# A decoder's cross-attention pieces beside its gated attention: the pairs of pieces moved by one

## The chip, the cores and the metric

The kernel runs on one core of one Trainium2 chip. The metric is the device time of one execution in microseconds (us), the median of the runs shown. The core's engines are TensorE (PE in the profile, PEld its weight loads), VectorE (DVE), ScalarE (ACT), GpSimd (POOL) and SyncE (SP), which issues the transfers. Each runs its own instructions in program order and meets the others at semaphores.

## The reference

A decoder of two layers on 8 sequences of 256 tokens, width 512, all float32. Each layer is attention, cross-attention to a context, and experts, each followed by a residual sum and a layer norm:

```python
x = _layernorm(x + _L0_attn_ref(x, Wq, Wk, Wv, Wg, Wc, bc))
x = _layernorm(x + _L0_xattn_ref(x, ctx_2048, ctx_2048))
x = _layernorm(x + _L0_ffn_ref(x, ...))
...
```

The change touches the first two. The first (called A here) squares the scores of 16 query heads and weights them by a gate, in blocks of 256 tokens here (one per sequence):

```python
qk = jnp.einsum("bthd,bshd->bhts", q, k) * scale
a = jnp.where(causal, qk ** 2 * jnp.exp(gate), 0.0)
y = jnp.einsum("bhts,bshd->bthd", a, v) / (jnp.sum(a, axis=-1) + 1e-06)
out = y.reshape(B, T, H * R * D) @ Wc + bc
```

The second (called C) has 16 heads of width 32, and takes the context as keys and values without a projection:

```python
scores = jnp.einsum("bhqd,bhkd->bhqk", q, kj) * SCALE
scores = jnp.where(causal, -inf, scores)
exp_c = jnp.exp(scores - scores.max(axis=-1, keepdims=True))
out = jnp.einsum("bhqk,bhkd->bhqd", exp_c / exp_c.sum(axis=-1, keepdims=True), vj)
```

## The kernel before

The program is seven stages: constants, `attention0` (A), `cross0` (C), and four more. A and C are written as generators: each engine's part of the stage yields after every tick, and `decoder` deals the ticks out by a list `order` of (stage, number of ticks). `in_order` (L159) runs that list for the banks of PSUM and for each of the five engines, so the list sets the order of work on every engine at once. No scheduler moves anything afterwards.

**A** has 32 steps n (8 pairs of heads, 4 groups of 512 tokens, in two halves) and two more that drain it. A step has 8 ticks on TensorE: three projections `project(n, m)` (L384, 12 matmuls each; ScalarE copies the high part qkH at L561, VectorE the rest qkL at L684); then two ticks of `out(n-2, ...)` (L417, 12 matmuls each, added to xN by VectorE at L653); then `attend(n-1)` (L434 to L439), in three late steps of the stage with 96 matmuls of values (L457) behind it; then `scores(n)` (L471, L473; ScalarE squares them at L597, VectorE multiplies them by the gate at L710); then `turn(n-1)` (eight transpositions at L486; ScalarE takes the high part yH at L605, VectorE the rest yL at L722). ScalarE also exponentiates the gates (L572) behind the third projection, and in every second step copies the next weights there (L575).

**C** has 8 batches j of 8 pieces i, a piece being two heads, and 16 ticks to a batch: 144 ticks in all, from -8 to 135. On an even tick 16j + 2i stand the scores of piece i, on the odd tick after it the transpositions of its exponentials. What belongs to a piece:

- `scores(j, i)`, TensorE L946: 12 matmuls into two banks. They wait until ScalarE has read the piece whose banks they take.
- VectorE L1061: four instructions that add the mask and take the maxima (each followed by a read of the accumulator).
- ScalarE L1030 and L1032: four exponentials into P, of which there is one copy (also with accumulator reads).
- `flip(j, i)`, TensorE L958: six transpositions of P, which wait for the exponentials, and for both banks 6 and 7.
- ScalarE L1040: the copy of the transposed P into PT.
- `attend(j, g)`, TensorE L929: once in two pieces, on the even ticks 4, 8, 12 and 16 of a batch ahead of the scores of that tick: 16 narrow matmuls of PT with the context. It waits for the copy (L1040) of the flip on the tick just before it. ScalarE copies the result at L1017.

Three times or less in a batch an even tick has more behind its scores: `turn` (L978, four transpositions of xN, ticks 16j - 6 and 16j + 6; ScalarE L1009, VectorE L1072) and `finish` (L968, tick 16j + 18; VectorE L1087). They too put their result into bank 6 or 7. The keys of C are split on GpSimd (L1119, L1121), and its context is loaded by SyncE.

Steps 0 to 16 of A run alone with all eight banks. From step 17 on A has banks 0 to 3, and C has 4 and 5 for scores and 6 and 7 for the rest: after every four ticks of A (behind the first out tick, and behind turn) come two of C, 66 in all. These places are called the half after out and the half after turn. What is then left of A and C follows, C alone:

```python
A, C, done = 1, 2, 0
order = [(0, 1), (A, 1 + 8 * 17)]
for n in range(17, 34):
    for ticks in (4, 4):
        beside = min(2, 66 - done)
        order += [(A, ticks), (C, beside)]
        done += beside
order += [(A, 2), (C, c0.ticks - done)]
```

Of the kernel before, what the change touches and what calls it, by code (L numbers as in the profile page):

```python
# [144 lines left out]
def whole(stage):  # L145

    def once(f):
        def pieces(e):
            f(e)
            yield  # L150
        return pieces

    def banks():
        yield

    return Stage(1, banks, *(once(f) for f in stage))


def in_order(order, pieces):  # L159
    for s, n in order:  # L160
        for _ in range(n):
            next(pieces[s])
    for s in pieces:
        assert next(s, None) is None
# [85 lines left out]
def constants(K):  # L250

    def gpsimd(e):
        step = K.steps(e, "pool_step")
        e.memset(K.onesF[:, :], 1.0)
        e.memset(K.onesel[:, :, :], 0.0)
        step(e.memset(K.idF[:, :], 0.0))
        step(e.affine_select(out=K.idF[:, :], in_=K.idF[:, :], compare_op=ALU.not_equal, fill=1.0, base=0,
                             pattern=[[-1, 128]], channel_multiplier=1))
        e.tensor_copy(K.idB[:, :], K.idF[:, :])
        for i in range(4):  # L260
            last = e.memset(K.onesel[:, i, i:i + 1], 1.0)
        last.then_inc(K.consts.sem, 1)

    nothing = lambda e: None
    return nothing, nothing, nothing, gpsimd, nothing
# [2774 lines left out]
def decoder(nc, d, out):  # L3040
    with ExitStack() as ctx:
        K = Kit(nc, ctx, d, out)
        first = whole(constants(K))
        a0 = attention0(K, 17)
        c0 = cross0(K)
        K.rooms, rooms = Rooms(), K.rooms
        rest = [whole(stage(K)) for stage in (experts0, attention1, cross1, experts1)]
        stages = [first, a0, c0, *rest]

        A, C, done = 1, 2, 0  # L3050
        order = [(0, 1), (A, 1 + 8 * 17)]
        for n in range(17, 34):
            for ticks in (4, 4):
                beside = min(2, 66 - done)
# [3 lines that stand above are left out]
        order += [(i, 1) for i in range(3, 7)]  # L3058

        block = ctx.enter_context(nc.Block())  # L3060
        in_order(order, [s.banks() for s in stages])

        @block.tensor
        def _(e):
            in_order(order, [s.engines[0](e) for s in stages])

        @block.scalar
        def _(e):
            in_order(order, [s.engines[1](e) for s in stages])

        @block.vector
        def _(e):
            in_order(order, [s.engines[2](e) for s in stages])

        @block.gpsimd
        def _(e):
            in_order(order, [s.engines[3](e) for s in stages])

        @block.sync
        def _(e):  # L3080
            in_order(order, [s.engines[4](e) for s in stages])
# [48 lines left out]
```

## Time and profile before

| | us |
|---|---|
| median of 2 runs | 2661.53 (2659.25 to 2663.8) |
| the profiled execution | 2657.87 |
| its span, first to last instruction | 2656.1 |
| TensorE busy in the span | 2206.7 (83%) |
| A alone (steps to 16) | about 25 to 430 |
| A and C together; the first transposition of exponentials starts at 470.0 | about 430 to 991 |
| C alone | about 991 to 1275 |

1.8 us of the profiled execution lie outside of its span. Times in the rows are microseconds from the start of the span. The granted clock is TensorE's, as a share of 2.4 GHz: 1.00 is that level, 0.50 is 1.2 GHz, and a value between is a mean over a stretch that had both. "Idle before" is the time for which the engine did nothing ahead of an instruction, with the instruction of another engine that ended it. Matmuls overlap: one has a duration of its own, but the next starts before it ends, so that a group's busy time is less than count times duration. A row of a stretch begins with its limits and length; then, engine by engine (PE, PEld, DVE, ACT, POOL), busy us and the count of instructions; then the granted clock, the share of the DMA engines and GB/s. For one line alone only PE and PEld stand there. A row of a timeline has the start, the us from the first start to the last end of the instructions merged in it, and the instruction.

### The profile page before, as it was taken

The page shows a single profiled execution, that of the slowest core. Times are in us where ns is not written, and L with a number is a line of the kernel's source. Part 1 is how long each engine was busy: PE and PEld are TensorE (multiplying, and loading weights), DVE is VectorE, ACT ScalarE, POOL GpSimd, SP SyncE. Part 2 cuts the span into 40 slices and gives each one's busy share as a digit, 9 for nine tenths or more (in the row PEclk, how much of TensorE's full clock was granted, in tenths as well). Part 3 has the DMA queues.
Part 4 walks back from the last instruction along what each step waited for, and adds up shares of the span by engine and source line. Part 5 has one row for each costly group of instructions (what it writes and reads, how often), then busy time and mean ns, then how long its engine had stood idle before and what let it go on. Part 6 is the DMA issues. An engine that isn't in the chain of part 4 may idle for free.

```text
span 2656.1 us, 37210 instructions
## 1 busy us (share of the span) xinstructions
PE 2206.7 (83%) x13669; PEld 1754.7 (66%) x13669; DVE 1251.9 (47%) x3209; ACT 1044.3 (39%) x2330; POOL 744.3 (28%) x668
## 2 busy tenths in 40 slices
PE   6999998877878865555789999998899978888774
PEld 6788887766767653444678888886665536666542
DVE  2644456333343343232531111333677767677655
ACT  3333233333333334333322111123466656777632
POOL 2734343223222210010024343003435432232110
PEclk9999999888888885555999999999899988999986
DMA  4211111011011000000100100001323330000001
GB/s 154 97 45 30 58 48 64 26 32 47 16 40 32 11 15 16 18 17 3 52 32 30 42 33 0 24 1 22 66 45 59 58 105 21 13 25 8 2 9 63
DMA packets 53173, 98.52 MB, mean 37 GB/s; under 512 B 6913, under 2 KB 31233, under 8 KB 50177
## 3 DMA queue, kind: packets, MB, share of 16 engines
q1 hardware_dynamic: 52992, 96.14, 12.7%
q8 instruction: 110, 1.80, 0.3%
q14 instruction: 71, 0.57, 0.1%
HBM read 75.61 MB, written 4.26 MB: 30 GB/s over the span
## 4 chain that ended last, share of the span: by engine, by line
PE 39%; issue 9%; DVE 8%; ACT 6%; POOL 2%; DMA 1%; SPq 0%; ACTq 0%; DVEq 0%; POOLq 0%
PE PS L1253 13%; PE PS L1325 3%; PE PS L1352 3%; PE PS L1736 2%; PE PS L1832 2%; PE PS L958 2%; PE PS L946 2%; DVE aM L1969 1%; PE PS L1800 1%; ACT xP L2494 1%; DVE st L191 1%; ACT cP L1032 1%; PE PS L2346 1%; PE PS L929 1%; ACT cP L1030 1%
## 5 line engine op out<-in xcount | busy, mean ns | idle before, releaser
L958 PE MATMUL PS<-idF,cP 128*128 128x128 f32 x384 | 94.3, 416 | 203.3 <-ACT cP L1032 186.9
L958 PEld LDWEIGHTS PS<-idF,cP 128*128 128x128 f32 x384 | 70.8, 215 | 219.2 <-issue 135.3
L1253 PE MATMUL PS<-WH,bXH 128*128 128x512 f32 x512 | 201.2, 393 | 5.4 <-POOL WL L1546 5.4
L1253 PE MATMUL PS<-WL,bXH 128*128 128x512 f32 x512 | 200.7, 392 | 0.0
L1253 PE MATMUL PS<-WH,bXL 128*128 128x512 f32 x512 | 200.7, 392 | 0.0
L1969 DVE TENSOR_REDUCE aM<-PS 128x4 f32<-128x1024 f32 x128 | 153.8, 1221 | 57.4 <-PE PS L1800 56.5
L1061 DVE CUSTOM_DVE_ANT_0 PS<-PS,cBAR 128x128 f32<-128x128 f32 (+1 forms) x256 | 83.7, 389 | 187.2 <-PE PS L946 187.2
L1456 DVE SCALAR_TENSOR_TENSOR s<-s,cf,PS 128x256 f32<-128x256 f32 x112 | 53.8, 481 | 249.0 <-ACT s L1371 240.0
L384 PE MATMUL PS<-aXH,QKH 128*128 128x512 f32 x384 | 162.4, 423 | 6.7 <-ACT sq L597 3.4
L684 DVE TENSOR_TENSOR qkL<-PS,qkH 128x512 fp32r<-128x512 f32 x96 | 65.8, 690 | 203.2 <-ACT qkH L561 203.2
L1371 ACT ACTIVATE s<-PS 128x256 f32<-128x256 f32 x128 | 49.0, 383 | 277.4 <-PE PS L1253 277.4
L384 PE MATMUL PS<-aXL,QKH 128*128 128x512 f32 x384 | 157.9, 411 | 0.0
L384 PE MATMUL PS<-aXH,QKL 128*128 128x512 f32 x384 | 156.9, 409 | 0.0
L653 DVE TENSOR_TENSOR xN<-PS,xN 128x512 f32<-128x512 f32 x128 | 88.3, 691 | 142.3 <-PE PS L417 139.1
L1908 ACT ACTIVATE aPT<-PS 128x1024 f32<-128x1024 f32 x128 | 128.6, 1024 | 50.7 <-PE PS L1820 49.7
L1561 POOL TENSOR_TENSOR mixed<-mixed,s 128x256 f32<-128x256 f32 x112 | 82.4, 739 | 183.3 <-DVE s L1456 183.3
L2494 ACT ACTIVATE xP<-PS,xM 128x256 f32<-128x256 f32 x256 | 118.0, 483 | 28.9 <-DVE xM L2616 28.9
L561 ACT ACTIVATE qkH<-PS 128x512 fp32r<-128x512 f32 x96 | 56.9, 598 | 173.9 <-PE PS L384 173.9
L710 DVE TENSOR_TENSOR aT<-sq,E 128x512 f32<-128x512 f32 (+1 forms) x128 | 88.6, 733 | 77.0 <-ACT sq L597 48.0
L597 ACT ACTIVATE sq<-PS 128x768 f32<-128x768 f32 x64 | 51.9, 811 | 163.8 <-PE PS L473 108.9
L417 PE MATMUL PS<-CH,yH 128*128 128x512 f32 x256 | 112.4, 439 | 3.4 <-DVE qkL L684 3.4
L1253 PEld LDWEIGHTS PS<-WH,bXH 128*128 128x128 f32 x512 | 97.0, 189 | 25.3 <-issue 5.5
(405 smaller groups left out, 6294.5 us busy)
## 6 DMA issues: line engine op xcount, KB each, us to landing
gQK<-in_Wqk SPq DMA_DIRECT2D x16, 768.0 KB, 6.3
gC<-in_Wc SPq DMA_DIRECT2D x16, 512.0 KB, 5.4
lgB<-gate_sums SPq DMA_DIRECT2D x32, 256.0 KB, 4.2
sg<-in_gu SPq DMA_DIRECT2D x8, 1024.0 KB, 5.0
aqs<-aQH SPq DMA_DIRECT2D x64, 128.0 KB, 4.3
xN<-in_xT SPq DMA_DIRECT2D x4, 1024.0 KB, 10.7
xN<-in_x SPq DMA_DIRECT2D x4, 1024.0 KB, 7.6
cst<-in_cT SPq DMA_DIRECT2D x8, 512.0 KB, 3.7
```

Of the source, the lines that this page charges most:

```text
L384: mm = e.matmul(PS[:, b, :], w[:, kc, 128 * m:128 * m + 128], x[:, kc, c:c + 512], start=kc == 0 and i == 0, stop=kc == KC - 1 and i == 2)
L417: mm = e.matmul(PS[:, b, :], y[:, h, 128 * i:128 * i + 128], w[:, h, :], start=h == 0 and k == 0, stop=h == 1 and k == 2)
L653: e.tensor_tensor(xN[:, t, :], PS[:, b, :], xN[:, t, :], ALU.add).then_inc(o_add.sem, 1)
L710: at = e.tensor_tensor(aT[:, j, c:c + w].rearrange("p (h q) -> p h q", h=2), sq[:, c:c + w].rearrange("p (h q) -> p h q", h=2), E[:, j:j + ...
L958: mm = e.transpose(PS[:, b + a, 128 * c:128 * c + 128], P[:, a, c, :], idF[:, :])
L1061: last_ = e.tensor_tensor_reduce(out=s, in0=s, in1=BAR[:, 256 - 128 * q:384], scale=1.0, scalar=3.0e38, op0=ALU.add, op1=ALU.min, accum_ou ...
L1253: mm = e.matmul(PS[:, b, :], x[:, kc, 128 * t:128 * t + 128], w[:, kc, :], start=kc == 0 and i == 0, stop=kc == KC - 1 and i == 2)
L1325: mm = e.matmul(PS[:, b + a, :], x[:, kc, 128 * t:128 * t + 128], w[:, kc, :], start=kc == 0 and i == 0, stop=kc == KC - 1 and i == 2)
L1561: e.tensor_tensor(mixed[:, t, :], mixed[:, t, :], s2[n % 2][:, 0:256], ALU.add).then_inc(t_add.sem, 1)
L1908: e.activation(PT[:, n % 8, :, :], PS[:, b:b + 2, :], ACTF.Exp, scale=0.25).then_inc(t_exp.sem, 1)
L1969: e.tensor_reduce(M[j % 2][:, :, :].rearrange("x q (h c) -> x h q c", h=2)[:, :, :, i], PS[:, b:b + 2, :].rearrange("p h (q k) -> p h q k" ...
L2494: last = e.activation(P[:, i % 2, a, q, :], PS[:, r, 256 * q:256 * q + 256], ACTF.Exp, bias=M[y][:, q, h:h + 1], scale=-1.0, accum_out=den ...
```

## The change

The list of ticks changes in two places. One tick of C (its first, -8) is placed ahead of step 17 of A, and the count of ticks placed starts at 1. So each pair of C ticks within the stage now begins with an odd tick: the transposition of piece i (with what its tick holds), then the even tick with the attend, if there is one, and the scores of piece i + 1. There are 32 pairs and one single tick instead of 33 pairs, 66 ticks as before. An even tick comes one half of a step of A earlier than before, an odd tick in the same half. No instruction is added or taken away.

```diff
-        A, C, done = 1, 2, 0
-        order = [(0, 1), (A, 1 + 8 * 17)]
+        A, C, done = 1, 2, 1
+        order = [(0, 1), (A, 1 + 8 * 17), (C, 1)]
         for n in range(17, 34):
             for ticks in (4, 4):
                 beside = min(2, 66 - done)
```

TensorE in the half after turn, before: the turn of A, the scores of a piece, its own flip, the first projection of A's next step.

```order
L486 MATMUL PS<-idF,yN 128x128 x8
L946 MATMUL PS<-cKH,cQH 128x128 x2
L946 MATMUL PS<-cKL,cQH 128x128 x2
L946 MATMUL PS<-cKH,cQL 128x128 x2
L946 MATMUL PS<-cKH,cQH 128x256 x2
L946 MATMUL PS<-cKL,cQH 128x256 x2
L946 MATMUL PS<-cKH,cQL 128x256 x2
L958 MATMUL PS<-idF,cP 128x128 x6
L384 MATMUL PS<-aXH_52,QKH 128x512
```

The same engine and place after the change.

```order
L486 MATMUL PS<-idF,yN 128x128 x8
L958 MATMUL PS<-idF,cP 128x128 x6
L929 MATMUL PS<-cPT,cV 32x256 x4
L929 MATMUL PS<-cPT,cV 32x128 x4
L946 MATMUL PS<-cKH,cQH 128x128 x2
L946 MATMUL PS<-cKL,cQH 128x128 x2
L946 MATMUL PS<-cKH,cQL 128x128 x2
L946 MATMUL PS<-cKH,cQH 128x256 x2
L946 MATMUL PS<-cKL,cQH 128x256 x2
L946 MATMUL PS<-cKH,cQL 128x256 x2
```

The flip moved ahead of the scores, and is now that of the piece before. The attend (L929), which stood in the half after out, came to the half after turn, right behind the flip whose copy it reads.

ScalarE around the same place, before: A's squares and yH, the exponentials of the piece, the copy of its flip, then A's qkH of the next step.

```order
L597 ACTIVATE sq<-PS 128x768 x2
L605 ACTIVATE yH<-PS 128x512 x2
L1030 ACTIVATE cP,cden_96<-PS,cM_94 128x128
L1032 ACTIVATE cP,cden_96<-PS,cM_94 128x256
L1030 ACTIVATE cP,cden_96<-PS,cM_94 128x128
L1032 ACTIVATE cP,cden_96<-PS,cM_94 128x256
L1040 ACTIVATE cPT<-PS 128x768
L561 ACTIVATE qkH<-PS 128x512 x3
```

ScalarE there after the change.

```order
L597 ACTIVATE sq<-PS 128x768 x2
L605 ACTIVATE yH<-PS 128x512 x2
L1040 ACTIVATE cPT<-PS 128x768
L1017 ACTIVATE cnT<-PS 128x256
L1030 ACTIVATE cP,cden_96<-PS,cM_94 128x128
L1032 ACTIVATE cP,cden_96<-PS,cM_94 128x256
L1030 ACTIVATE cP,cden_96<-PS,cM_94 128x128
L1032 ACTIVATE cP,cden_96<-PS,cM_94 128x256
L561 ACTIVATE qkH<-PS 128x512 x3
```

The copy L1040 moved ahead of the exponentials, with L1017 behind it; both stay behind A's squares and yH.

TensorE in the half after out, in a pair whose even tick has a finish, after the change: the end of A's first out tick, the flip, the scores, and the finish (L968) behind them; the next row is A's second out tick.

```order
L417 MATMUL PS<-CH,yL 128x512
L958 MATMUL PS<-idF,cP 128x128 x6
L946 MATMUL PS<-cKH,cQH 128x128 x2
L946 MATMUL PS<-cKL,cQH 128x128 x2
L946 MATMUL PS<-cKH,cQL 128x128 x2
L946 MATMUL PS<-cKH,cQH 128x256 x2
L946 MATMUL PS<-cKL,cQH 128x256 x2
L946 MATMUL PS<-cKH,cQL 128x256 x2
L968 MATMUL PS<-idF,cnT 128x128 x8
L417 MATMUL PS<-CH,yH 128x512
```

All turns and finishes of C within the stage stand in this half now, behind a flip whose banks 6 and 7 they take one of.

## Rows read from the trace of the kernel before

**Rows 1.** The page: span, busy time, TensorE and its granted clock in 40 slices.

```profile
span 2656.1 us, 37210 instructions
PE 2206.7 (83%) x13669; PEld 1754.7 (66%) x13669; DVE 1251.9 (47%) x3209; ACT 1044.3 (39%) x2330; POOL 744.3 (28%) x668
...
PE   6999998877878865555789999998899978888774
...
PEclk9999999888888885555999999999899988999986
```

**Rows 2.** Busy time by stretch: A alone, both together, C alone.

```profile
200.00:430.00 230.00, 227.69 (x1295) 197.67 (x1293) 118.17 (x230) 74.63 (x117) 97.40 (x79) 1.00 0.16 48
...
467.00:989.00 522.00, 412.90 (x2456) 346.28 (x2453) 204.20 (x560) 172.49 (x426) 127.43 (x107) 0.87 0.09 28
989.00:1260.00 271.00, 155.22 (x1000) 114.37 (x998) 80.69 (x373) 102.02 (x345) 24.73 (x24) 0.51 0.04 13
```

**Rows 3.** Waits from 467 to 989: total us, times, longest.

```profile
PE PS L958 <- ACT cP L1032: 96.1, 26, 6.2
...
PE PS L958 <- DVE coN L1087: 11.9, 3, 4.0
```

**Rows 4.** Busy time by stretch of one line alone: L384, then L417, then L958.

```profile
200.00:430.00 230.00, 86.24 (x360) 66.80 (x360) 1.00 0.16 48
467.00:989.00 522.00, 118.53 (x432) 93.55 (x432) 0.87 0.09 28
...
200.00:430.00 230.00, 59.76 (x255) 47.43 (x253) 1.00 0.16 48
467.00:989.00 522.00, 104.68 (x340) 79.14 (x341) 0.87 0.09 28
...
467.00:989.00 522.00, 41.30 (x174) 30.85 (x174) 0.87 0.09 28
```

**Rows 5.** Timeline of one half after turn: start, us, instruction.

```profile
564.72 1.04 PE L486 MATMUL PS<-idF,yN 128*128 128x128 f32 x8
...
565.69 0.33 PE L946 MATMUL PS<-cKH,cQH 32*128 32x128 f32 x2
...
566.29 1.08 ACT L605 ACTIVATE yH<-PS 128x512 fp32r<-128x512 f32 x2
566.36 0.28 PE L946 MATMUL PS<-cKH,cQL 32*128 32x256 f32 x2
...
568.63 0.29 DVE L1061 CUSTOM_DVE_ANT_0 PS<-PS,cBAR 128x128 f32<-128x128 f32 x1
...
570.60 0.48 ACT L1032 ACTIVATE cP<-PS,cM 128x256 f32<-128x256 f32 x1
...
571.31 1.48 PE L958 MATMUL PS<-idF,cP 128*128 128x128 f32 x6 [4.08 <-ACT cP L1032]
...
573.02 0.63 PE L384 MATMUL PS<-aXL,QKH 128*128 128x512 f32 x1
...
575.46 0.39 PE L384 MATMUL PS<-aXH,QKL 128*128 128x512 f32 x1
```

**Rows 6.** Timeline: the waits of two flips in the half after out.

```profile
660.23 1.51 PE L958 MATMUL PS<-idF,cP 128*128 128x128 f32 x6 [2.74 <-ACT cP L1032]
...
860.98 1.04 PE L958 MATMUL PS<-idF,cP 128*128 128x128 f32 x6 [2.74 <-ACT cP L1032]
```

**Rows 7.** C alone: the waits of the attends, and a flip, its copy and its attend.

```profile
PE PS L929 <- ACT cPT L1040: 18.1, 18, 1.0
...
1063.97 0.81 ACT L1040 ACTIVATE cPT<-PS 128x768 f32<-128x768 f32 x1 [1.75 <-PE PS L958]
1064.88 1.51 PE L929 MATMUL PS<-cPT,cV 128*32 128x256 f32 x16 [1.01 <-ACT cPT L1040]
```

**Rows 8.** Timeline of a half after out: ScalarE's last work of A, the attend.

```profile
617.85 1.48 ACT L575 ACTIVATE QKH<-gQK 128x1536 fp32r<-128x1536 f32 x1
...
619.14 0.86 PE L929 MATMUL PS<-cPT,cV 128*32 128x256 f32 x16
```

## The prediction

> **What bounds the kernel now.** The page comes first: TensorE is busy for 83% of the span, more than any other engine, but its row of slices has a dip from the eighth slice on, and the row of the granted clock has eights in the same slices, where it had nines before [rows 1]. A slice is 66 us, so that is where A and C run together. The view by stretches says it in numbers. In A alone TensorE is busy for 227.7 of 230 us at a clock of 1.00; from 467 to 989 us it is busy for 412.9 of 522 us at 0.87; in C alone for 155.2 of 271 us at 0.51 [rows 2]. In the middle stretch VectorE has 204, ScalarE 172 and GpSimd 127 us of work in 522, so none of them is full. What TensorE waits for there stands in the view of waits: the flips, L958, for ScalarE's exponentials, 96.1 us in 26 waits, and for VectorE's coN, 11.9 us in 3 [rows 3]. That is 108.0 us in 29 waits, one for each of the 174 / 6 = 29 flips of the stretch [rows 4]. Nothing else of size stands in the way.
>
> The timeline of one half shows why. The scores end at about 566.64 us. VectorE is still at A's work and starts the maxima at 568.63; the last exponential ends at 570.60 + 0.48 = 571.08; only then does the flip go, after 4.08 us of idle [rows 5]. In the half after out VectorE is free and the wait is 2.74 us [rows 6]. Every piece thus pays a trip through VectorE and ScalarE in full, though TensorE has A's work ready behind it.
>
> **What the waits cost beside themselves.** Behind such a wait matmuls of A take 0.63 us, some microseconds later 0.39 us again [rows 5]: these are the two levels of the clock, 1.2 and 2.4 GHz. I price it from busy time for each matmul. L384: 118.53 / 432 = 0.274 us in the middle stretch against 86.24 / 360 = 0.240 in A alone, times 432: 15 us. L417: 104.68 / 340 = 0.308 against 59.76 / 255 = 0.234, times 340: 25 us. The flips: 41.30 / 29 = 1.42 us each, against 1.04 for one at the full level, times 29: 11 us [rows 4, 6]. Together 51 us, or 1.8 us for each wait.
>
> **What the change removes.** The flip of piece i now stands four ticks of A behind its scores. The trip took 571.08 - 566.64 = 4.4 us with VectorE's backlog in it [rows 5]. The cover after the half after turn is three projections and an out tick: 48 matmuls at 0.23 us, 11 us. After the half after out it is an out tick, 12 x 0.234 = 2.8 us, and A's attend, scores and turn. In A alone 360 / 36 = 10 steps left (227.7 - 86.2 - 59.8) / 10 = 8.2 us each for these three and the values [rows 2, 4]; about half of it is theirs, so the cover is some 7 us. Both exceed 4.4 us, and the 7 us still do with the copy of the flip (0.81) added, which ScalarE now makes before the exponentials [rows 7]. So the 29 waits go, 108 us. At the end of the stage A's steps are short: its last two have no projections, and a flip there has only an out tick of 2.8 us as cover. I leave 2 us for this (bounds 0 and 6, two waits of 2.74 us [rows 6]).
>
> **What it adds: the attend behind its flip.** Before, the attend began its pair and found the copy of the last flip long done; it starts at 619.14 with no idle ahead of it [rows 8]. Now flip, copy and attend follow one another. C alone has this very order, and there each attend waits, 18.1 us in 18 waits, 1.0 us each, with TensorE's flips at the lower clock [rows 7]. Beside A it is worse, for all attends have come to the half after turn, where ScalarE has A's yH before the copy. Step by step from rows 5: turn ends at 564.72 + 1.04 = 565.76; a flip at the full level then ends at about 566.7 (the 1.04 of rows 6, begun while the turn drains); yH ends at 566.29 + 1.08 = 567.37; the copy takes 0.81 and the attend starts 0.10 after it (1064.88 - 1063.97 - 0.81) [rows 7]: 568.3. The wait is 1.6 us. Attends stand on every fourth tick from 4 to 56, 14 of them: 22 us. Bounds: 14 x 1.0 = 14 us, as in C alone, and 14 x 2.4 = 34 us if ScalarE is a square (0.8 us) later than in the row. Behind the waiting attend are queued the scores and then A's projections; ScalarE's exponentials and VectorE's maxima wait for these scores, but nothing needs them before the next half.
>
> **What it adds: banks 6 and 7.** The 7 turns and 3 finishes of C in the stage now stand behind a flip and 12 matmuls of scores (565.69 to 566.64, 0.95 us), and need a bank that the copy frees [rows 5]. In the half after out ScalarE is free at 617.85 + 1.48 = 619.33 at the latest, before the flip would end at about 620.0 [rows 8]. The copy ends 0.9 us after the flip (0.10 + 0.81), so against 0.95 us of scores little is left: 0.4 us each with a second hop, 4 us in 10 (bounds 0 and 10 us).
>
> **What it adds: lags in A.** ScalarE's exponentials now fall into A's first projection. With the attend from 568.3 on (0.8 us until the scores start) and 0.95 us of scores, these end at about 570.1. From the first maximum to the last exponential it took 571.08 - 568.63 = 2.45 us [rows 5], so ScalarE is free at about 572.7. The projection ends at 570.1 + 2.8 = 572.9, and qkH is not late. That is 0. But the margin is 0.2 us, and a denser TensorE leaves less slack in steps with norms and values. The other bound is VectorE's backlog in the row, 568.63 - 566.64 = 2.0 us, in each of 17 steps: 34 us. I stay near the row that I followed, and take 6 us.
>
> The transfers move by half a step with their ticks, against batches of 16 ticks; SyncE's and GpSimd's items of C come no later relative to those who need them. At nothing: GpSimd's 127 us of work in 522 leave it room [rows 2]. If a key load came late, TensorE would wait at the scores.
>
> **The clock after the change.** Waits of 2.74 us and more were followed by the lower level; whether 1.6 us are is not shown. Bounds: never, 0 us, or each as dear as now, 14 x 1.8 = 25 us. The place has only short matmuls around the wait (turn, flip, attend, scores), so I take half, 12 us. Of the 51 us, 39 come back.
>
> On the flips themselves the rows are plain: of two flips after the same wait one took 1.51 us and one 1.04 us, so transpositions do run at the upper level [rows 6]. The Trainium skill, "TensorE: Matmul & The Clock Gate", section on PE-mode transpose, speaks against a gain here: it says that the full clock does not engage for transpositions. By that rule flips would stay at 1.51 us, and the change would return 11 us less; by the rows it returns them. The trace disagrees with the page, and I go by the trace.
>
> **The sum.** 108 + 51 = 159 us are there to win. Taken back: attends 22, banks 6 and 7 4, the end of the stage 2, A's lags 6, clock 12, together 46. The gain is 113 us. C alone and all later stages keep their order and their time. Against the profiled execution: 2657.87 (span 2656.1 and 1.8 around it) - 113 = 2544.9 us. The median of the runs is 3.7 us above that execution, so 2661.53 - 113 = 2548.5, and I predict 2548 us. All terms at their good ends give 108 + 51 - 14 = 145 us, 2517; at their bad ends 159 - 34 - 10 - 6 - 34 - 25 = 50 us, 2611. All bad at once is unlikely; the likeliest case alone spans 2522 to 2590.
>
> **Rivals.** *The clock stays down.* The wait of 1.6 us stands between transpositions and narrow matmuls, and a lower level may follow each time and last twice as long as now. For it: in C alone, made of the same instructions, the clock is 0.51 throughout [rows 2]. Against it: 11 us of dense matmuls follow each time. Price: 14 x 3.6 = 50 us instead of 12: 2548 + 38 = 2586 us.
>
> *The attend hardly waits.* If ScalarE is through with yH when the flip ends, each attend waits 1.0 us as in C alone, the clock stays up, and banks and lags cost nothing: 159 - 14 - 2 = 143 us, 2518. For it: the one row of this place that I followed need not be typical. Against it: rows 5, where the copy cannot start before 567.37.
>
> *The wait only moves.* A's projections find their banks not free, since qkH and qkL come behind the exponentials in both engines' queues, and L384 or L417 wait as long as L958 did. Then only the 4 ticks' distance is spent, and the time is 2661 less some 10: 2650. For it: just four banks. Against it: 7 and 11 us of cover over a trip of 4.4.
>
> *Slower.* The same mechanism at full strength, and the attend's wait on top. Place: A's out blocks, which wait for qkL's bank. Price: all 108 + 51 us stay, plus 14 x (1.6 + 1.8) = 48 us: 2661 + 48 = 2709. It decides once the lag per half exceeds the cover of at least 7 us by more than 3.7 us, a trip of about 11 us, more than double the 4.4 of rows 5. It would need a queue that I do not see.
>
> **Chances.** The forecast 0.74, the clock staying down 0.13, the attend hardly waiting 0.08, the wait moved 0.03, slower 0.02. The range takes in the first three cases nearly whole: 2515 to 2595 us. What a measurement can tell from no change is about 2%, 53 us, so faster means below 2608: all of the first three cases, 0.95; same is the moved wait, 0.03; slower 0.02.
>
> **What would show it.** Right: in the stretch of A and C together, now about 410 us long instead of 522, waits of L958 for cP near nothing; 14 waits of L929 for cPT of about 1.6 us; a mean clock of 0.95 or more; L384 near 0.24 us of busy time for each matmul; the stretch of C alone still 271 us. The first rival shows as a clock under 0.92 with the waits gone, the second as waits of L929 near 1.0 us, the third as waits of L384 or L417 for sq, qkL or xN of over 2 us in each half. The forecast is wrong if flips still wait, if C alone grows, or if some other line waits for over 30 us in sum.

## The result, and the profile after

| | before | after |
|---|---|---|
| median of the runs | 2661.53 (2 runs) | 2530.47 (2529.7 to 2531.25) |
| ratio, 95% interval | | 0.9508 (0.9467 to 0.9549) |
| the same with more runs, on another chip | 2649.86 (7 runs) | 2530.27 (4 runs), 0.9548 (0.9534 to 0.9563) |
| span of the profiled execution | 2656.1 | 2528.0 |

The forecast was 2548 us with a range of 2515 to 2595. The gain is 131 us in the first comparison and 120 in the second: the kernel before is at 2650 to 2655 us in all later comparisons, and the changed one at 2530 in both.

The page of the changed kernel, the rows that answer to [rows 1]:

```profile
span 2528.0 us, 37196 instructions
PE 2157.2 (85%) x13655; PEld 1717.9 (68%) x13669; DVE 1247.5 (49%) x3209; ACT 1043.3 (41%) x2330; POOL 746.3 (30%) x668
...
PE   7899999999899755657899999997999877888774
...
PEclk9999999999999955559999999997999999999886
```

The eights in the clock before its four fives are gone, and TensorE's row has nines, with one eight, up to the place where C is alone. By stretch, against [rows 2]:

```profile
200.00:430.00 230.00, 227.08 (x1291) 196.84 (x1290) 118.29 (x230) 74.44 (x117) 97.91 (x78) 1.00 0.15 48
430.00:860.00 430.00, 397.14 (x2592) 335.51 (x2592) 218.62 (x586) 179.19 (x435) 142.59 (x121) 0.98 0.12 39
...
867.00:1130.00 263.00, 149.35 (x976) 110.26 (x978) 77.84 (x368) 102.01 (x345) 23.16 (x22) 0.51 0.05 14
```

A alone is the same. Where both run, TensorE is busy for 92% instead of 79% of the time, and its clock is 0.98 instead of 0.87. C alone is the same, at 0.51. The view of one line gives first and last start of its instructions, and so the ends of the stages: A's last out block, and C's last attend.

```profile
L417 PE MATMUL PS<-CH,yL x256: 388/389/398, 88.5 to 866.8; 128*128 128x512 f32 x128
...
L929 PE MATMUL PS<-cPT,cV x512: 271/421/635, 477.4 to 1130.5; 128*32 128x128 f32 x86, 128*32 128x256 f32 x85
```

Before, A's last matmul started at 991.8 and C's last attend at 1255.4. So A ends 125.0 us earlier (866.8), C alone takes 263.7 us instead of 263.6, and everything behind it takes 1397.5 instead of 1400.7 us. Of the 128.1 us between the two spans 125.0 were made where the change is. TensorE's whole work from 430 us to the end of A's last out block, before and then after:

```profile
430.00:992.20 562.20, 448.22 (x2624) 374.95 (x2624) 227.10 (x610) 186.68 (x449) 142.02 (x122) 0.88 0.10 30
```

```profile
430.00:867.20 437.20, 403.93 (x2624) 340.52 (x2624) 223.65 (x608) 184.55 (x448) 142.59 (x121) 0.98 0.12 39
```

The same 2624 matmul records take 44.3 us less of busy time, and the idle time falls from 114.0 to 33.3 us, 80.7 less: together the 125.0 us.

All waits of TensorE for another engine from 430 to 867 us, against [rows 3]:

```profile
PE PS L929 <- ACT cPT L1040: 27.6, 14, 3.4
...
PE PS L384 <- ACT sq L597: 1.4, 1, 1.4
PE PS L434 <- DVE xN L653: 1.3, 1, 1.3
PE PS L417 <- DVE qkL L684: 1.1, 1, 1.1
PE PS L486 <- DVE yN L664: 0.8, 1, 0.8
PE PS L958 <- ACT cP L1032: 0.2, 1, 0.2
```

Of 108 us of waits of the flips 0.2 are left. In their place stand 14 waits of the attends. One half after turn, against [rows 5]:

```profile
567.28 1.03 PE L486 MATMUL PS<-idF,yN 128*128 128x128 f32 x8
568.15 0.82 PE L958 MATMUL PS<-idF,cP 128*128 128x128 f32 x6
568.18 0.81 ACT L597 ACTIVATE sq<-PS 128x768 f32<-128x768 f32 x1 [1.15 <-DVE aT L710]
...
568.88 1.08 ACT L605 ACTIVATE yH<-PS 128x512 fp32r<-128x512 f32 x2
...
569.84 0.83 ACT L1040 ACTIVATE cPT<-PS 128x768 f32<-128x768 f32 x1
...
570.77 0.86 PE L929 MATMUL PS<-cPT,cV 128*32 128x256 f32 x16 [1.80 <-ACT cPT L1040]
571.55 0.33 PE L946 MATMUL PS<-cKH,cQH 32*128 32x128 f32 x2
```

The flip goes at once and is done at 568.97. ScalarE has A's square and yH ahead of the copy, which ends at 570.67, and the attend starts 0.10 us later: 1.80 us of wait. Of the 14, eleven are 1.76 to 1.94 us, two 3.43, and the last 1.01.

Busy time of one line alone by stretch, L384, L417 and L958, against [rows 4]:

```profile
430.00:860.00 430.00, 125.69 (x504) 98.81 (x504) 0.98 0.12 39
...
430.00:860.00 430.00, 88.52 (x360) 66.37 (x360) 0.98 0.12 39
...
430.00:860.00 430.00, 22.91 (x168) 19.59 (x168) 0.98 0.12 39
```

For each matmul that is 0.249 us in L384 (0.274 before, 0.240 in A alone) and 0.246 in L417 (0.308 and 0.234). A flip of six takes 0.82 us, where 1.42 stood before.

### The profile page after: what moved, and what is told of

Same layout as the page of the kernel before. It is cut to its first block, busy times and chain, and to the rows that moved or that the text cites. A ratio compares the mean times of both kernels' runs of the same rounds, so it can differ in the third digit from the quotient of the medians.

```text
span 2528.0 us, 37196 instructions
## 1 busy us (share of the span) xinstructions
PE 2157.2 (85%) x13655; PEld 1717.9 (68%) x13669; DVE 1247.5 (49%) x3209; ACT 1043.3 (41%) x2330; POOL 746.3 (30%) x668
## 4 chain that ended last, share of the span: by engine, by line
PE 47%; issue 9%; DVE 9%; ACT 6%; POOL 2%; DMA 1%; SPq 0%; ACTq 0%; DVEq 0%; POOLq 0%
PE PS L1253 14%; PE PS L1325 3%; PE PS L1736 3%; PE PS L384 2%; PE PS L1832 2%; PE PS L1352 2%; PE PS L946 2%; PE PS L958 2%; PE PS L417 2%; DVE aM L1969 1%; PE PS L1800 1%; ACT xP L2494 1%; DVE st L191 1%; PE PS L929 1%; ACT cP L1032 1%
## 5 line engine op out<-in xcount | busy, mean ns | idle before, releaser
L384 PE MATMUL PS<-aXH,QKH 128*128 128x512 f32 x384 | 156.5, 408 | 4.3 <-POOL QKL L771 2.6
L958 PE MATMUL PS<-idF,cP 128*128 128x128 f32 x384 | 76.7, 356 | 95.7 <-ACT cP L1032 91.2
L384 PE MATMUL PS<-aXH,QKL 128*128 128x512 f32 x384 | 153.5, 400 | 0.0
L384 PE MATMUL PS<-aXL,QKH 128*128 128x512 f32 x384 | 153.3, 399 | 0.0
L958 PEld LDWEIGHTS PS<-idF,cP 128*128 128x128 f32 x384 | 60.2, 185 | 108.4 <-issue 71.0
L710 DVE TENSOR_TENSOR aT<-sq,E 128x512 f32<-128x512 f32 (+1 forms) x128 | 85.5, 709 | 76.9 <-ACT sq L597 47.9
L757 POOL TENSOR_SCALAR E<-lgB,lgS 128x256 f32<-128x256 f32 x64 | 73.2, 1143 | 128.5 <-DVE aT L710 118.7
```

The lines of the kernel that those rows point to most:

```text
L384: mm = e.matmul(PS[:, b, :], w[:, kc, 128 * m:128 * m + 128], x[:, kc, c:c + 512], start=kc == 0 and i == 0, stop=kc == KC - 1 and i == 2)
L710: at = e.tensor_tensor(aT[:, j, c:c + w].rearrange("p (h q) -> p h q", h=2), sq[:, c:c + w].rearrange("p (h q) -> p h q", h=2), E[:, j:j + ...
L958: mm = e.transpose(PS[:, b + a, 128 * c:128 * c + 128], P[:, a, c, :], idF[:, :])
```

## The experiments

The theory: the gain is the waits of the flips and the lower clock behind them; the attends' waits are the price, and both are a matter of distance between a piece of work and what it waits for. The rivals are named in each expectation. Ratios are to the kernel before in the same comparison, with their 95% intervals.

**Half a step early, pairs unchanged.** Two ticks of C ahead of step 17 instead of one.

```diff
-        A, C, done = 1, 2, 0
-        order = [(0, 1), (A, 1 + 8 * 17)]
+        A, C, done = 1, 2, 2
+        order = [(0, 1), (A, 1 + 8 * 17), (C, 2)]
```

> The pairs stay as before (scores, then their own flip), but two ticks of C stand ahead of step 17, so that every tick of C comes half a step of A earlier. Theory (the waits of the flips and the clock behind them are the whole gain): the 29 waits stay, about 108 us in sum, and the time stays at 2661 us within 10. Rival (C's earlier place is worth something, since the change brought half of C's ticks forward): a good part of the 131 us appears here too, a time below 2620 us.

Measured: 2642.6 us, ratio 0.9956 (0.9939 to 0.9973): 9 us less by the medians, 12 by the ratio (7 to 16). The waits of L958 from 430 to 977 us:

```profile
PE PS L958 <- ACT cP L1032: 93.3, 26, 6.0
PE PS L958 <- DVE coN L1087: 6.1, 3, 2.0
```

They stay, so the earlier place alone does not remove them. But the place is worth something too: the waits for coN fall from 11.9 to 6.1 us, and those for A's squares from 3.4 to 0.7, probably since C's turns and finishes now meet another half of A's step. About a tenth of the gain would be had without swapping anything; it is of the same kind, and I had counted the coN waits among the 108 us.

**The waits filled.** The kernel before with matmuls of the identity ahead of the flip's wait. The fill was 12 of them at all 29 flips, then 6, then 6 at only the 19 flips whose banks are free at once:

```diff
             for w in left:
                 e.wait_ge(*w)
+            if 8 * j + i < 29 and i not in (3, 5) and not (i == 1 and j):
+                for _ in range(6):
+                    e.matmul(PS[:, b, 0:128], idF[:, :], idF[:, :], start=True, stop=True)
             e.wait_ge(*s_exp.upto(8 * j + i + 1))
```

> The kernel before, with 12 float32 matmuls of the identity with itself put into the flip's bank ahead of each wait of the 29 flips that stand beside A (the flip overwrites them; nothing else is changed). TensorE waits for the same exponentials, but is not idle for most of it. Theory (half-rate matmuls behind the waits cost 48 to 57 us): the flips start no earlier, the granted clock of the stretch rises from 0.87 to 0.95 or more, and the time falls by 30 to 55 us, to 2606 to 2630 us. Rival (A's matmuls are slower in this stretch for another reason, as the other engines' traffic to PSUM and SBUF): no change or a loss, 2661 us or more.

> As e2, with 6 matmuls of the identity instead of 12. In e2 twelve took 4.47 us and ended 3.7 us after the exponentials were done (2.0 us were expected of them), so that the flips were late; the clock rose from 0.87 to 0.93 all the same. Six take 2.2 us, less than the shortest wait (2.74). Theory (the clock behind the waits costs about 50 us): the flips start no later, the clock of the stretch is 0.93 or more, and 25 to 50 us come back, 2601 to 2626 us. Rival: the identity matmuls keep the clock up only in the half after out, where nothing holds their bank: 10 to 25 us. If nothing comes back, the clock term of the prediction was wrong and the 48 us were something else.

> As e7 (6 identity matmuls ahead of the wait, 1.61 us at the full level), but only at the 19 of 29 flips whose banks are free at once. In e7 the other ten waited 4.1 us for VectorE's cQL or coN first and then had the fill on top, some 16 to 22 us, beside a gain of 12. Theory (half rate behind the waits costs about 1.7 us each): 19 x 1.3 to 1.8 = 25 to 34 us come back and nothing is added, 2616 to 2626 us. Rival (the clock term is worth little, and e7's stretch was shorter by chance of the clock's phase): 2640 us or more.

Measured: 12 at all flips, 2649.0 us, ratio 0.9991 (0.9979 to 1.0003). 6 at all, 2637.4 us, 0.9946 (0.9932 to 0.9961). 6 where free, 2631.4 us, 0.9917 (0.9885 to 0.9950). The first fill was mis-sized: each identity matmul counts as two and twelve took 4.47 us in one half. Its time did not fall, but its rows settle the question that it was for. Busy time of L384, then L417, from 467 to 980 us:

```profile
467.00:980.00 513.00, 106.13 (x432) 83.64 (x432) 0.93 0.09 28
...
467.00:980.00 513.00, 82.61 (x336) 61.90 (x336) 0.93 0.09 28
```

That is 0.246 us for a matmul of either line, as after the change (0.249 and 0.246), with C's work in the order of before (0.274 and 0.308). From 430 us to the end of A, L384, L417 and L958 together are busy for 293.4 us before, 241.9 with this fill and 243.9 after the change. So nearly all of the slower matmuls came from the idle time ahead of them; the rival, another cause of slow matmuls in this stretch, is out. What the fill gave back it lost again by its own length.

Where a turn of C has the flip's bank, even six are late (timeline of the second kernel; ScalarE's last exponential ends at 566.17, the fill after 568.2):

```profile
564.94 0.69 DVE L1075 SCALAR_TENSOR_TENSOR cQL<-PS,cQH 128x512 fp32r<-128x512 f32 x1
...
565.68 2.56 PE L957 MATMUL PS<-idF 128*128 128x128 f32 x12 [3.39 <-DVE cQL L1075]
565.69 0.48 ACT L1035 ACTIVATE cP<-PS,cM 128x256 f32<-128x256 f32 x1
```

The time of the second kernel is in the range of its rival, but not for the rival's reason: L384, which follows the other half, is faster too (0.253 us). In the third kernel nothing is late; a fill and its flip:

```profile
500.10 1.61 PE L957 MATMUL PS<-idF 128*128 128x128 f32 x12
502.83 0.88 PE L961 MATMUL PS<-idF,cP 128*128 128x128 f32 x6 [1.12 <-ACT cP L1035]
```

Work that computes nothing, put into a wait that stays, saves 22 us (13 to 31), or 1.2 us for each of 19 waits. I had expected 25 to 34. Behind 15 of the 19 the remaining idle was 1.1 to 1.3 us, and no matmul of A ran at the lower level before the next wait. At the other four 3.1 to 3.9 us of idle remained, and 7 or 8 matmuls of A behind them were slow again. So the lower clock behind a wait is a cost of its own, and the clock term of the prediction is real.

**The attend further from its copy.** The changed kernel twice: with the attend behind the scores of its tick on TensorE, and one tick later (`batch(tick, 4)` becomes `batch(tick, 5)` for the banks, TensorE and ScalarE), so that it opens the next pair.

```diff
-            j, r = batch(tick, 4)
+            j, r = batch(tick, 5)
             if r >= 0 and r % 4 == 0:
```

> The changed kernel, with the attend issued behind the scores of its tick on TensorE and not ahead of them. Theory (the 14 attends beside A wait 1.8 us, two of them 3.4, for the copy behind A's yH on ScalarE, 27.6 us): 12 matmuls of scores, 0.95 us, now cover part, the waits fall by some 13 us to about 14, and in C alone 18 waits of 1.0 us go too, where scores take about 1.6 us, though there the scores' own trip bounds: 2530 - 13 - (0 to 18) = 2499 to 2517 us. Rival (TensorE is not the bound there, the time is made by ScalarE's queue): 2525 to 2535 us.

> The changed kernel, with the attend one tick later: it opens the next pair, ahead of the flip, and its copy is a half step old. Theory: all 14 waits beside A go (27.6 us) with the 3 to 5 us of half-rate matmuls behind them, and in C alone the attends fill the wait of the flip for its exponentials: 18 waits of about 1.0 us and their 0.8 to 1.5 us of work, 18 to 40 us. Together 2530 - 30 - (18 to 40) = 2460 to 2482 us. Rival (the wait moves on, to the flip's banks or to A's banks): 2505 us or more, with a wait of another line of about 2 us, 14 times.

Measured: behind the scores 2488.8 us, ratio 0.9380 (0.9362 to 0.9398); a tick later 2472.2 us, 0.9319 (0.9292 to 0.9346). The first is faster than I had expected, the second as expected. Waits of TensorE beside A in the first (430 to 853 us), then in the second (430 to 849):

```profile
PE PS L929 <- ACT cPT L1040: 15.2, 13, 2.6
```

```profile
PE PS L958 <- ACT cnT L1017: 8.1, 14, 1.0
PE PS L417 <- issue: 3.7, 2, 2.1
PE PS L384 <- ACT sq L597: 3.0, 3, 1.4
```

The sum falls from 27.6 to 15.2, as the 0.95 us of scores say (13 of them, 12.4 us), and then goes, with 8.1 us of a new wait for the bank that the attend's result leaves. A's last matmul starts 14.5 and 18.1 us earlier than after the change. In C alone more came back than I had expected of the first: 236.5 and 224.5 us instead of 263.7. There TensorE waits for the trip of each piece, so all that stands on it lengthens the stage: taking the attend and its wait off it is worth 39 us for 18 attends.

**The same in the kernel before.**

> The kernel before, pairs as they were, with the attend one tick later: behind the scores of its pair and ahead of the flip, with a copy that is old. Beside A the attend of 0.8 us now lies inside the flip's wait (14 times, up to 11 us), in C alone 18 waits of 1.0 us go, and the attend's 1.5 us move into the flip's wait. Theory (in C alone each piece is a trip through VectorE and ScalarE, and what TensorE does meanwhile is free): C alone gives the same 28 to 32 us as in e3 and e4, in all 30 to 45 us, 2606 to 2620 us. Rival (e3's and e4's gain in C alone came from the shifted pairs): 2640 us or more.

Measured: 2605.2 us, ratio 0.9827 (0.9809 to 0.9845). C alone takes 224.6 us here too, 39 less where I had expected 28 to 32, with the pairs unchanged. So that part has nothing to do with the shift.

**Single ticks.** The kernel before with C's ticks one at a time.

```diff
-            for ticks in (4, 4):
-                beside = min(2, 66 - done)
+            for ticks in (2, 2, 2, 2):
+                beside = min(1, 66 - done)
```

> The kernel before, with one tick of C after every two of A instead of two after every four; the same 66 ticks beside A, the first at the same place. A flip stands two ticks of A behind its scores (3.1 or 5.5 us of TensorE's work), an attend two ticks behind its flip. Theory (distance, not the swapped pair, is what counts, and the attend's wait is a matter of distance too): 108 + 48 us come back but for flips with only A's scores and turn as cover (14 of them, 0 to 2 us each), and no attend waits: 2651 - 156 + (0 to 30) = 2495 to 2525 us, below the changed kernel. Rival (A's own chain of scores, square, gate, attend and turn gets in the way when C's work stands inside it): 2540 us or more, with waits of L434, L471 or L486.

Measured: 2528.5 us, ratio 0.9539 (0.9523 to 0.9555), the same as the change; the expectation was 2495 to 2525. TensorE's waits from 430 to 859 us:

```profile
PE PS L486 <- ACT sq L597: 11.9, 13, 1.2
PE PS L384 <- ACT sq L597: 8.3, 14, 2.3
PE PS L958 <- ACT cP L1032: 5.4, 2, 3.8
PE PS L929 <- ACT cPT L1040: 4.2, 2, 3.2
```

The theory holds for the flips and the attends: 5.4 and 4.2 us of waits, with no pair swapped. The swapped pair is thus one way to the distance, and not the only one. The rival holds in part, at places that I had not named: C's work ahead of A's turn and projections makes these wait for the squares' banks, 20 us. And what follows C took 1404.0 us here against 1397.5, which hides 6 of the 8 us by which A's last matmul is earlier (858.6 against 866.8).

**Why two attends wait 3.4 us.** The changed kernel, with the copy L554 moved into the next step:

```diff
-                next_values(v)
+                if not v:
+                    next_values(v)
             yield
...
             for m in range(3):
+                if m == 0 and events.get(n - 1):
+                    next_values(events[n - 1])
```

> The changed kernel, with ScalarE's copy of A's next value weights (L554, 1.06 us) moved from its place ahead of the squares into the next step. Of the 14 waits of L929, 12 are 1.8 us and two 3.4, in the two steps that have this copy. Theory (the attend waits for whatever ScalarE has of A ahead of the copy cPT): these two fall to 1.8 to 2.4 us, the sum from 27.6 to 25 or less, and the time by 2 to 5 us. Rival (the two long waits come from the values' matmuls or VectorE's copies of them): the sum stays at 27.6.

Measured: 2527.3 us, ratio 0.9531 (0.9508 to 0.9555), within the noise of the change. The wait itself is what was to be read:

```profile
PE PS L932 <- ACT cPT L1043: 24.7, 14, 1.9
```

It falls as expected, and the longest is 1.9 us, but not by the path that I had given. The timeline of the changed kernel in such a half:

```profile
509.78 1.06 ACT L554 ACTIVATE VH<-gV 128x1024 fp32r<-128x1024 f32 x1 [1.09 <-PE PS L457]
...
510.83 0.81 ACT L597 ACTIVATE sq<-PS 128x768 f32<-128x768 f32 x1
510.98 2.39 POOL L791 TENSOR_TENSOR VL<-gV,VH 128x1024 fp32r<-128x1024 f32 x1 [20.92 <-ACT VH L554]
...
511.73 2.52 DVE L710 TENSOR_TENSOR aT<-sq,E 128x512 f32<-128x512 f32 x2 [1.58 <-ACT sq L597]
...
514.28 0.81 ACT L597 ACTIVATE sq<-PS 128x768 f32<-128x768 f32 x1 [2.64 <-DVE aT L710]
```

ScalarE lost little by its own copy. The copy released GpSimd's subtraction L791, and beside it VectorE's two instructions of L710 took 2.52 us instead of 1.03; the second square waited for these, and the attend's copy for the square. In the kernel with the copy moved, L791 is gone from this place and the same pair is short:

```profile
511.41 1.03 DVE L713 TENSOR_TENSOR aT<-sq,E 128x512 f32<-128x512 f32 x2 [1.58 <-ACT sq L600]
```

The pair is 1.49 us shorter, and so is the attend's wait, 1.94 us instead of 3.43.

**The same rule in C alone.** From the kernel with the attend a tick later: in C alone a flip is issued behind the scores of the next piece, with scores in banks 0 to 3 and the rest in 4 to 7; then also the attend between the next scores and the next flip.

```diff
-            j, r = batch(tick, 0)
-            if r >= 0 and r % 2 == 0:
-                scores(j, r // 2)
-            elif r >= 0:
-                flip(j, r // 2)
+            for lag in ((2, 0) if tick < 58 else (0, 2)):
+                j, r = batch(tick, lag)
+                if r >= 0 and r % 2 == 0:
+                    (flip if lag else scores)(j, r // 2)
```

> e4 (the changed kernel with the attend a tick later), and in C alone the same thing that the change does beside A: a flip is issued behind the scores of the next piece, which take banks 0 to 3 in turn, and flips and the rest take banks 4 to 7, since A has left them. Beside A nothing differs from e4 but the tick that a flip is counted under. Theory (in C alone each piece pays a trip of scores, VectorE, ScalarE, flip and copy, 7.7 us for a piece before, and distance hides it as beside A): with scores and maxima ahead, a piece is ScalarE's exponentials (2.1), the flip (1.3 at the lower level), the copy (0.9) and hops, 4.5 to 5 us for 35 pieces, so that some 80 to 100 us go: 2472 - 90 = 2370 to 2395 us. Rival (C alone is bound by TensorE at the lower clock or by GpSimd's key splits): 2440 us or more.

> e8 with the attend, in C alone, between the scores of the next piece and the flip, not right behind the flip whose copy it reads. In e8's C alone (182 us, before 264) that wait is 18 times 1.0 us. Theory (the same rule once more: keep a piece of work away from what it waits for): 18 us go, and some of the lower clock with them (it is 0.63 there), 2429 - 18 to 35 = 2394 to 2411 us. Rival (in e8 ScalarE's copy and exponentials make the period, and TensorE's wait only moves to the next flip): 2420 us or more, with the flips' waits for cP up by as much.

Measured: 2429.3 us, ratio 0.9154 (0.9130 to 0.9179), and 2423.7 us, 0.9139 (0.9116 to 0.9161). Both beat the change by about 100 us. C alone takes 182 us in the first (from 847.9 to 1030.2). That is 42 us less than with the attend moved alone, half of what I expected, and the expected time was missed. Neither that theory nor its rival was right in full: by stretch and by waits (848 to 1031 us) in the first,

```profile
848.00:1030.00 182.00, 132.55 (x984) 101.49 (x987) 80.19 (x368) 99.15 (x345) 23.21 (x22) 0.60 0.07 20
```

```profile
PE PS L961 <- ACT cP L1043: 23.4, 12, 8.8
PE PS L932 <- issue: 12.1, 12, 1.0
PE PS L949 <- DVE cQL L1077: 7.9, 4, 2.4
PE PS L932 <- ACT cPT L1012: 6.0, 6, 1.0
```

TensorE is busy for 133 of 182 us at a clock of 0.60: its own work, most of it at the lower level, has become the larger part of a piece. In the second kernel the 18 attend waits go but for one (1.0 us), yet L961 waits 29.5 us instead of 23.4 and the finish 6.0 us for cnT; the intervals of the two ratios overlap. The time is in the range of the rival named there. The wait moved to the next flip only in part: of the 17 us that the attends gave up 6 came back there and 6 at the finish.

## Why the prediction was right, point by point

- **The waits of the flips go: right.** 107.9 us, 0.2 left. The trip of 4.4 us was that of one half: the flip with the longest wait (6.2 us) started 6.8 us behind the end of its scores (970.4 to 977.2). Even such trips were covered; the waits of over 5 us stand in the half after turn, where the cover was put at 11 us. The 2 us left for the end of the stage were not needed.
- **The attend's wait: right in its place and cause, too small.** 14 waits, as counted. 1.6 us each was forecast, 1.80 measured in the ordinary halves. The failing number is the end of the flip: I took 1.04 us for it from [rows 6]; at the upper level it is 0.82, so TensorE is at the wait earlier. I did not see the two waits of 3.4 us, in the steps where GpSimd's L791 holds up VectorE. 27.6 us instead of 22. Moving the attend showed that the wait is what it costs, since 12.4 us less of it ended A 14.5 us earlier.
- **Banks 6 and 7: 4 us forecast, nothing measured.** No turn or finish of C stands in the view of waits.
- **Lags in A: 6 us forecast.** L384, L434, L417 and L486 wait 4.6 us together after, 5.9 before over the same steps (3.4, 1.7 and 0.8). Net nothing, and no sign of the rival of a moved wait.
- **The clock: the term is real, what came back was undersized.** By the same busy times, the excess over the upper level was 15 us in L384, 25 in L417 and, with 0.82 for a flip, 17 in the flips: 57 us. After it is 504 x (0.249 - 0.240) = 5 and 360 x (0.246 - 0.234) = 4 us. 48 us came back in these lines, not 39. The clock did fall behind 5 of the 14 new waits, but the price in these lines is 9 us, not 12, and the flips gave 6 us more than forecast. The kernel with twelve fills shows cause and size: the same lines lose 51 us of busy time there. TensorE's busy time as a whole fell by 44 us with the change; the lines overlap, and L946 and L929 took 1.7 us more.
- **Transpositions at the upper level: right.** A flip takes 0.82 us after the change; before, most took 1.51 (1.42 in the mean). The page "TensorE: Matmul & The Clock Gate" of the Trainium skill, section on PE-mode transpose, has it that the full clock does not engage for transpositions; for flips amid A's matmuls the trace disagrees. Whether transpositions alone would bring the clock up, no run here shows. The rows that I used (1.51 against 1.04) still hid part of the gain.
- **C alone: right.** 263.6 us before and 263.7 after. The 271 of the prediction is the length of my row's stretch, which took in a little of its neighbours.
- **The sum:** the forecast was 113 us. In the stretch of A and C the idle time fell by 81 us (108 less 27.6 for the attends, and small change) and the busy time by 44: 125 us. Another 3 us of the 128 between the spans lie behind C, where nothing was changed. The mechanism was right; the number is 12 us short in this stretch, because I had put small costs on several things that cost nothing and undersized what the clock returns. The larger wait of the attends hid some 6 us of that. The 131 us between the first medians flatter the change: beside the 120 of the comparison with more runs the forecast is short by 7.
- **The rivals' prices:** the slower case, 2709 us, is 1.8% above the kernel before, so by my own line of 2% a measurement would have called it the same.

## What to carry to other kernels

Where two stages share an engine in slots, it matters less how much work a slot holds than how far apart in issue order a result and its consumer stand: swapping two ticks removed 108 us of waits and moved no work. Look at every consumer that the swap brings close to its producer; here the attend came right behind its flip, and one tick more of distance was worth another 58 us, 18 of them beside A and 39 in C alone, where the swap plays no part. Count a wait twice where the clock falls behind it, once as idle and once as slow work.

## What the runs showed of the hardware that I had not expected

- Of the eleven waits of TensorE of 1.8 to 1.9 us among short matmuls, eight left A's next matmuls at 0.39 us, the upper level, and three were followed by matmuls of 0.63 us, the lower one. Both of 3.4 us, and all 29 of 2.74 us and more in the kernel before, were followed by 0.63 us.
- Filling a wait with matmuls that compute nothing made the kernel faster, ratio 0.9917 (0.9885 to 0.9950).
- VectorE's L710 (two inputs in SBUF) took 2.52 us for the pair beside GpSimd's L791 and 1.03 us elsewhere, and ended 0.88 us after it. The Trainium skill, "SBUF — State Buffer", section "Who interferes with whom", says that the two share a pair of ports which one instruction holds to its end; the trace agrees.
- The program behind C, which is the same in all kernels, took between 1391.9 and 1404.0 us by which kernel ran ahead of it. The granted clock differs in places there: in the kernel before it is 0.95 and then 0.87 in the last two stretches (from 2200 and from 2400 us), in the changed one 0.97 and 0.85 in the same places of the program. A difference of 5 us between two kernels says little here about the part that was changed; the ends of the stages in the trace say more.
